# Four gated layers on one core: layer 3's expert rows written plainly to rows of their own and added at the end, and layer 0's router fed from the normalised rows

## What is computed

```
layer 0:  x += tanh(g) * attention(normalised x)                 # 4 sequences of 256
          probs = softmax(norm(x) @ gate_w.T); top 8 of 64 experts, at most 128 tokens each
          x += tanh(g) * sum over the 8 of  prob * expert(norm(x))
layer 3:  mixing with a state space (as in layer 1)
          score = sigmoid(norm(x) @ gate_w.T); top 4 of 32 experts, no limit
          weights = softmax of the 4 logits
          x += tanh(g) * sum over the 4 of  weight * expert(norm(x))
          # expert e: (96 + 128) wide; its second part is shared by two experts
```

## Time and profile before

| | us |
|---|---|
| median of three timed runs (1319.25 to 1321.8) | 1319.86 |
| the profiled execution, device time | 1314.2 |
| its span, first to last instruction | 1312.4 |
| PE busy in the span | 1082.1 (82%) |
| DVE busy | 872.4 (66%) |
| POOL busy | 709.7 (54%) |
| ACT busy | 666.2 (51%) |
| POOL's gathers of layer 3 (L2385, x63) | 61.8 |
| POOL's scatters of layer 3 (L2376, x63) | 100.0 |

### The profile page before, as it was taken

How to read it: one execution, slowest core, us unless ns; L and a number is a source line. 1 busy time by engine, 2 the same in 40 slices (tenths; PEclk the granted TensorE clock), 3 DMA queues, 4 the chain that set the end, 5 groups by cost and what they waited for, 6 DMA issues and landing times.

```text
span 1312.4 us, 18185 instructions
## 1 busy us (share of the span) xinstructions
PE 1082.1 (82%) x5380; PEld 841.4 (64%) x5381; DVE 872.4 (66%) x1543; ACT 666.2 (51%) x1702; POOL 709.7 (54%) x480
## 2 busy tenths in 40 slices
PE   6646668887765988999999999799999737999992
PEld 3525656766623655888888888665555536888781
DVE  4645989898869895566566665859997782332221
ACT  4275245454464214787777777467662125333330
POOL 1002878888733223444554445429996105888873
PEclk9768789999977998999999999979999757999996
DMA  6391789988550003111011110305443992555556
GB/s 184 95 212 59 180 217 322 269 248 217 102 146 1 0 1 95 56 50 53 22 49 55 51 51 1 101 1 150 148 137 75 282 220 65 82 83 83 82 78 130
DMA packets 141109, 146.06 MB, mean 111 GB/s; under 512 B 34180, under 2 KB 127356, under 8 KB 141028
## 3 DMA queue, kind: packets, MB, share of 16 engines
q1 hardware_dynamic: 115556, 110.71, 29.2%
q0 software_dynamic: 24384, 33.31, 15.2%
q10 hardware_dynamic: 1088, 1.05, 0.2%
HBM read 119.04 MB, written 25.99 MB: 111 GB/s over the span
## 4 chain that ended last, share of the span: by engine, by line
PE 45%; POOL 15%; DVE 15%; issue 12%; ACT 6%; DMA 6%; SPq 0%; ACTq 0%; POOLq 0%; DVEq 0%
PE bank L1608 4%; PE bank L1671 4%; PE bank L1704 4%; PE bank L1693 4%; PE bank L2472 4%; POOL f_sums L1039 3%; POOL arena L1025 2%; PE bank L1597 2%; PE bank L2138 2%; PE bank L1626 2%; PE bank L1682 2%; POOL y L2385 2%; POOL arena L585 2%; DMA f_sums<-arena,put 2%; DMA e_sums<-ctxT,put 2%
## 5 line engine op out<-in xcount | busy, mean ns | idle before, releaser
L565 DVE TENSOR_TENSOR_SCAN arena<-arena 128x1024 f32<-128x1024 f32 x64 | 155.3, 2426 | 8.3 <-DVE arena L554 3.9
L1039 POOL DMA_INDIRECT f_sums<-arena,put x64 | 126.7, 1980 | 23.6 <-issue 17.7
L585 POOL TENSOR_TENSOR arena<-arena 128x1024 f32<-128x1024 f32 x32 | 82.4, 2575 | 89.7 <-DVE arena L565 89.7
L1025 POOL DMA_INDIRECT arena<-y_rows,slots x64 | 79.6, 1244 | 81.6 <-DVEq L1232 60.7
L2376 POOL DMA_INDIRECT e_sums<-ctxT,put x63 | 100.0, 1587 | 24.0 <-issue 15.5
L2472 PE MATMUL bank<-arena,ssm_y 128*128 x504 | 109.7, 362 | 2.2 <-issue 1.3
L543 ACT ACTIVATE arena<-arena,ssm_A 128x255 f32<-128x255 f32 x256 | 107.9, 498 | 1.7 <-DVE arena L487 1.5
L2138 PE MATMUL bank<-yT,arena 128*128 128x512 f32 (+1 forms) x224 | 105.8, 618 | 2.2 <-ACT arena L2069 2.2
L595 PE MATMUL bank<-arena,ident 128*128 128x256 f32 x256 | 69.3, 418 | 40.7 <-DVE arena L585 37.2
L554 DVE TENSOR_TENSOR arena<-arena 128x1024 f32<-128x1024 f32 x64 | 94.4, 1475 | 0.0
L2385 POOL DMA_INDIRECT y<-y_rows,slots x63 | 61.8, 982 | 59.6 <-DVEq L2656 40.7
(11 more groups left out here) (342 smaller groups left out, 2792.2 us busy)
## 6 DMA issues: line engine op xcount, KB each, us to landing
arena<-bc_rows SPq DMA_DIRECT2D x64, 512.0 KB, 5.4
arena<-in_L_ffn_w_gate_dram SPq DMA_DIRECT2D x16, 256.0 KB, 3.7
arena<-in_L_ffn_w_up_dram SPq DMA_DIRECT2D x16, 256.0 KB, 4.5
arena<-in_L_ffn_w_down_dram SPq DMA_DIRECT2D x16, 256.0 KB, 5.5
x<-in_L_ffn_w_gate_dram SPq DMA_DIRECT2D x16, 256.0 KB, 3.8
y<-in_L_ffn_w_up_dram SPq DMA_DIRECT2D x16, 256.0 KB, 4.4
yT<-in_L_ffn_w_down_dram SPq DMA_DIRECT2D x16, 256.0 KB, 6.1
arena<-in_L_ffn_Wd_dram SPq DMA_DIRECT2D x1, 3072.0 KB, 18.1
```

The lines of the kernel that those rows point to most:

```text
L565: nc.vector.tensor_tensor_scan(ssm_h[:, j % 2, :], ssm_decay[:, j % 2, :], ssm_in, 0.0, ALU.mult, ALU.add).then_inc(s_ssm_h, 1)
L585: ops.tensor_tensor(ssm_hC_buf[:, j % 2, :], ssm_h[:, j % 2, :], ssm_C[:, g % 2, :], ALU.mult).then_inc(s_ssm_hC, 1)
L1025: nc.gpsimd.indirect_dma_start(out=f0_xg[:, n % RING, e, :], out_offset=None, in_=y_rows, in_offset=bass.IndirectOffsetOnAxis(ap=slots[:, ...
L1039: nc.gpsimd.indirect_dma_start(out=f0_sums[m % SUMS], out_offset=bass.IndirectOffsetOnAxis(ap=put[:, m:m + 1], axis=0), in_=f0_ye[:, n % R ...
```

## The change

Two things are changed.

**Layer 3's sums.** e_sums is replaced by one DRAM tensor e_rows of 4 x 1024 + 64 x 128 rows. The table that PE makes holds 4 x token + k + 1 in place of the token's number; the product with the one-hot factor moves from ACT to DVE, since it differs over k. DVE first writes put and shifts it right by two for slots. Unused slots go to the rows behind the 4096. The scatter is a plain indirect DMA, and waits neither for the scatter of t - 2 nor for a first copy of x. The two clearing transfers for e_sums[1], the last rows of both, and the copy of x are gone. At the end SP reads 8 parts of 512 KB (4 neighbouring rows, 4 KB, for each partition), DVE makes three additions for each token tile (128x512, 128x256, 128x256), and SP stores 8 parts.

**Layer 0's router.** rows_turn and its logits leave the attention loop. The logits come from y after the normalisation, by norm_pe (four transposes, a copy by ACT and the products, for each pair of tiles, on banks 0 and 1) at the head of f0_pe; the scale rstd goes. The attention loop on DVE now runs two taps per sequence, behind the division instead of before it, and so all eight taps of both halves. ACT runs ssm_u_act and ssm_A_act straight behind the attention, ahead of the copies and the exponentials of the router.

```diff
@@ l0x_pe @@
             for b in range(B):
                 if b >= 2:
                     l0x_pe_energy(pe, b)
                 if b >= 1:
                     l0x_pe_out(pe, b - 1)
-                if b >= 2:
-                    rows_turn(b - 2)
             l0x_pe_out(pe, B - 1)
-            rows_turn(B - 2)
-            for b in range(B - 1):
-                rows_logits(b)
-            rows_turn(B - 1)
-            rows_logits(B - 1)
-            logits.last.then_inc(s_f0_logit, 1)
@@ l0x_act @@
-                if b >= 2:
-                    rows_turn_act(act, b - 2, 1, (6, 7))
             l0x_act_turn(act, B - 1)
-            for b in range(B - 2, B):
-                rows_turn_act(act, b, 1, (6, 7))
+            ssm_u_act(act, 0)
+            ssm_A_act(act)
@@ l0x_dve @@
-                ssm_conv_dve(dve, 0, 0, (b,))
                 dve.wait_ge(s_l0_exp, TPB * (b + 1))
...
                 last.then_inc(s_l0_att, 1)
+
+                ssm_conv_dve(dve, 0, b // 2, range(2 * (b % 2), 2 * (b % 2) + 2))
                 if b >= 1:
                     l0x_dve_add(dve, b - 1)
@@ f0_sp @@
-            for rows in f0_sums[1:] + e_sums[1:]:
+            for rows in f0_sums[1:]:
...
-            for rows in f0_sums + e_sums:
+            for rows in f0_sums:
@@ f0_pe @@
+            logits = pair_logits(bank[2], E0, gwT)
+            norm_pe(pe, 1, 1, logits)
+            logits.last.then_inc(s_f0_logit, 1)
             ssm_dt_pe(pe, 0)
@@ f0_act_eng @@
+            norm_act(act, 1)
             act.wait_ge(s_f0_top, 1)
...
-                                            bias=f0_top[:, i:i + 1], scale=rstd[:, i:i + 1], accum_out=f0_sum[:, i:i + 1])
+                                            bias=f0_top[:, i:i + 1], accum_out=f0_sum[:, i:i + 1])
             last.then_inc(s_f0_exp, 1)
-            ssm_A_act(act)
-            ssm_u_act(act, 0)
             ssm_dbl_act(act, 0)
@@ f0_dve @@
             norm_dve(dve, 1)
-            ssm_conv_dve(dve, 0, 1, range(DC))
@@ e_sp @@
-            sp.wait_ge(s_z_x, 2 * B)
-            sp.dma_start(e_sums[0][0:T, :].rearrange("(i p) d -> p i d", p=P), x[:, :, :]).then_inc(s_e_init[0], 16)
...
-            for b in range(B):
-                tiles = slice(TPB * b, TPB * (b + 1))
-                for dst, rows in ((x, e_sums[0]), (e_more, e_sums[1])):
-                    sp.dma_start(dst[:, tiles, :], rows[0:T, :].rearrange("(i p) d -> p i d", p=P)[:, tiles, :]
-                                 ).then_inc(s_e_more[b][0], 16)
+            for i in range(NT):
+                sp.dma_start(e_more[:, i, :, :], e_rows[i * P * K3:(i + 1) * P * K3, :].rearrange("(p k) d -> p k d", k=K3)
+                             ).then_inc(s_e_back[i][0], 16)
@@ e_pool, scatter(t) @@
                 wait(pool, s_e_ye, t + 1)
-                if t >= 2:
-                    wait(pool, s_e_st[(t - 2) % 4], 16 * ((t - 2) // 4 + 1))
-                if t == 0:
-                    wait(pool, s_e_init, 16)
                 nc.gpsimd.indirect_dma_start(
-                    out=e_sums[t % 2], out_offset=bass.IndirectOffsetOnAxis(ap=put[:, t:t + 1], axis=0),
-                    in_=e_ye[:, t % 4, :], in_offset=None, oob_is_err=True, compute_op=ALU.add).then_inc(s_e_st[t % 4][0], 16)
+                    out=e_rows, out_offset=bass.IndirectOffsetOnAxis(ap=put[:, t:t + 1], axis=0),
+                    in_=e_ye[:, t % 4, :], in_offset=None, oob_is_err=True).then_inc(s_e_st[t % 4][0], 16)
@@ e_act @@
-                nc.scalar.activation(e_rhs[:, i % 2, :, 0:TILES], e_ot[:, i % 2, :, :], ACT.Copy, scale=token_1[:, i:i + 1])
@@ e_dve @@
+                wait(dve, s_e_ot, i + 1)
+                V.tensor_tensor(e_rhs[:, i % 2, :, 0:TILES], e_ot[:, i % 2, :, :],
+                                e_tok[:, i, :].unsqueeze(2).to_broadcast([P, K3, TILES]), ALU.mult)
...
-            dve_link(V.tensor_scalar(slots[:, :], bank[5][:, 0:TILES], 1.0, 0.0, ALU.subtract, ALU.max))
+            dve_link(V.tensor_scalar(put[:, :], bank[5][:, 0:TILES], 1.0, 0.0, ALU.subtract, ALU.max))
+            dve_link(V.tensor_scalar(slots[:, :], put[:, :], K3.bit_length() - 1, None, ALU.logical_shift_right))
...
+            for i in range(NT):
+                wait(dve, s_e_back[i], 16)
+                four = e_more[:, i, :, :]
+                dve_link(V.tensor_tensor(four[:, 0:2, :], four[:, 0:2, :], four[:, 2:4, :], ALU.add))
+                dve_link(V.tensor_tensor(four[:, 0, :], four[:, 0, :], four[:, 1, :], ALU.add))
+                V.tensor_tensor(x[:, i, :], x[:, i, :], four[:, 0, :], ALU.add).then_inc(s_e_x[0], 1)
```

More of the change, by code:

```diff
@@ L710, in l0x_pe @@
             pe.wait_ge(s_sp_pad, 4)
-            logits = pair_logits(bank[2], E0, gwT)
-            def rows_turn(b):
-                pe.wait_ge(s_l0_x, b + 1)
-                rows_turn_pe(pe, b, 1, (6, 7))
-            def rows_logits(b):
-                pe.wait_ge(s_yT, NT // 2 + b + 1)
-                logits(b)
             for b in range(B):
@@ L843, in flamingo_kernel @@
         f0_sums = [nc.dram_tensor(f"f0_sums{e}", [T + CAP, D], F32, kind="Internal").ap() for e in range(SUMS)]
-        e_sums = [nc.dram_tensor(f"e_sums{e}", [T + CAP, D], F32, kind="Internal").ap() for e in range(2)]
+        e_rows = nc.dram_tensor("e_rows", [4 * T + E0 * CAP, D], F32, kind="Internal").ap()
         at = 0
@@ L919, in flamingo_kernel @@
         s_f0_clear = sem("s_f0_clear")
-        CLEARS = 8
+        CLEARS = 5
         s_f0_more = [sem(f"s_f0_more{b}") for b in range(B)]
@@ L944, in f0_const_pool @@
             nc.gpsimd.iota(iota_c[:, :], [[1, CAP]], base=0, channel_multiplier=0, allow_small_or_imprecise_dtypes=True)
+            nc.gpsimd.iota(e_tok[:, :, :], [[P * K3, NT], [1, K3]], base=1, channel_multiplier=K3,
+                           allow_small_or_imprecise_dtypes=True)
+            nc.gpsimd.iota(e_none[:, :], [[P, TILES]], base=K3 * T + 1, channel_multiplier=1, allow_small_or_imprecise_dtypes=True)
             nc.gpsimd.iota(token_1[:, :], [[P, NT]], base=1, channel_multiplier=1,
@@ L1187, in f0_dve @@
             norm_dve(dve, 1)
-            ssm_conv_dve(dve, 0, 1, range(DC))
             dve.wait_ge(s_f0_logit, 1)
-            dve_link(nc.vector.tensor_reduce(f0_top[:, :], bank[2][:, :].rearrange("p (i e) -> p i e", i=NT), AX_X, ALU.max,
-                                             negate=True))
-            nc.vector.tensor_tensor(f0_top[:, :], f0_top[:, :], rstd[:, :], ALU.mult).then_inc(s_f0_top, 1)
+            nc.vector.tensor_reduce(f0_top[:, :], bank[2][:, :].rearrange("p (i e) -> p i e", i=NT), AX_X, ALU.max,
+                                    negate=True).then_inc(s_f0_top, 1)
             dve.wait_ge(s_f0_exp, 1)
@@ L2277, in flamingo_kernel @@
         assert at <= ARENA
-        e_more = area(0, NT, D)
+        e_more = area(0, NT, K3, D)
         XR = 8
@@ L2328, in flamingo_kernel @@
         s_e_ld = (s_x_w[0], 16 * H // 2)
-        s_e_more = [(s, 16 * SUMS) for s in s_f0_more]
+        s_e_back = [(s, 16 * SUMS) for s in s_f0_more] + [(s, 16 * B * GB) for s in s_ssm_B + s_ssm_C]
         s_e_x = (s_f0_x, B)
+        e_tok = sb("e_tok", [P, NT, K3])
+        e_none = sb("e_none", [P, TILES])
         EL = 14
@@ L2654, in e_dve @@
             wait(dve, s_e_place, NT)
-            dve_link(V.tensor_scalar(slots[:, :], bank[5][:, 0:TILES], 1.0, 0.0, ALU.subtract, ALU.max))
+            dve_link(V.tensor_scalar(put[:, :], bank[5][:, 0:TILES], 1.0, 0.0, ALU.subtract, ALU.max))
+            dve_link(V.tensor_scalar(slots[:, :], put[:, :], K3.bit_length() - 1, None, ALU.logical_shift_right))
             dve.sem_inc(s_e_slots[0], 1)
-            dve_link(V.tensor_scalar(slot_none[:, :], bank[5][:, 0:TILES], 0.0, none_row[:, 0:1], ALU.is_equal, ALU.mult))
+            dve_link(V.scalar_tensor_tensor(out=slot_none[:, :], in0=bank[5][:, 0:TILES], scalar=0.0, in1=e_none[:, :],
+                                            op0=ALU.is_equal, op1=ALU.mult))
             V.scalar_tensor_tensor(out=put[:, :], in0=bank[5][:, 0:TILES], scalar=-1.0, in1=slot_none[:, :],
@@ L2681, in e_dve @@
             e_steps(dve, step)
-            for b in range(B):
-                wait(dve, s_e_more[b], 32)
-                rows = x[:, TPB * b:TPB * (b + 1), :].rearrange("p a n -> p (a n)")
-                more = e_more[:, TPB * b:TPB * (b + 1), :].rearrange("p a n -> p (a n)")
-                V.tensor_tensor(rows, rows, more, ALU.add).then_inc(s_e_x[0], 1)
+            for i in range(NT):
[4 more added lines that the diff above has]
+                V.tensor_tensor(x[:, i, :], x[:, i, :], four[:, 0, :], ALU.add).then_inc(s_e_x[0], 1)
         s_out = sem("s_out")
@@ L2693, in store_sp @@
             rows = out.rearrange("b (h p) d -> p (b h) d", p=P)
-            for b in range(B):
-                wait(sp, s_e_x, b + 1)
-                sp.dma_start(rows[:, TPB * b:TPB * (b + 1), :], x[:, TPB * b:TPB * (b + 1), :]).then_inc(s_out, 16)
-            sp.wait_ge(s_out, 16 * B)
```

(4 more changed lines are left out.)

1 line of the change is left out of this document (removed).

## The result

Timed beside each other nine times, the kernel after takes 1327.29 us in the median (1323.8 to 1329.12) and the kernel before 1320.34 (1318.62 to 1323.25): a ratio of 1.0045, with a 95% interval of 1.0033 to 1.0057. The forecast was 1305.6. On one of theirs, called E, the same two programs came to 1292.79 (two runs) and 1315.27 us, 0.9821 (0.976 to 0.9881).

A forecast was written before the change was run, and what follows sets the result against it. No engine is busy throughout; the chain of waits counts, in layer 3's experts on PE until 1189, then POOL. The terms -15.7 + 6.5 + 0.9 - 6.0 = -14.3 us take the median from 1319.9 to 1305.6, range 1299 to 1317.

The forecast's parts named there:

- Part 1: Layer 3's experts: a plain scatter costs POOL 0.99 us, not 1.59, and the last landing comes 15.7 us earlier.
- PE then keeps its pace.: Layer 3's experts: with POOL at 2.58 us a tile, PE holds 2.82, its last product ending at 1279.0.
- the gathers and the 32 pairs follow as before: Layer 0's experts: after the earlier routing this stage runs unchanged, so the -6.0 us is passed on.
- Part 2: The end of the kernel: reading back 4.2 MB for 2.1 MB adds 6.5 us after the last landing.
- late as feared: Reading back: last part in at +16.0 us, DVE about as late; loads alone at 244 GB/s would make it +9.5.
- Part 3: Layer 3's routing: DVE gains 0.42 us a tile, ACT loses 0.51; +0.9 us in all, bounds 0 and +2.
- Part 4: Layer 0's router: later logits but earlier Silu and state-space products, -6.0 us, bounds -4.6 and -9.3.
- a time before 83: Layer 0's routing: ACT's first tile, forecast at 85.3, coming this early would say PE had its full clock.
- A: Layer 3's experts: the plain scatter keeps its 1.59 us; total -2.6 us, 1317.3, chance 15%.
- C: Layer 3's experts: the plain write costs POOL more than the accumulating one; at 1.98 us, 1341.5; chance 4%.
- B: Layer 0 gives nothing, as something unseen holds the start of the pairs; total -8.3 us, 1311.6, chance 6%.
- D: Layer 3's experts: POOL is freed, but the four e_ye buffers still hold PE; no chance of its own.

The follow-up runs named there:

- e14: The kernel before, unchanged, run on chip E for its profile: 1316.46 us, 1.0007 of before.
- e17: The kernel after, unchanged, on chip E: 1292.79 us from two runs, 0.9821 of before.
- e12: The kernel before with compute_op=ALU.add left out of layer 3's scatter, so rows overwrite each other, on chip D: 1328.2 us, 1.0047 of before.
- e2: The kernel before with the product with the token's number (L2528) moved from ACT to DVE, on chip A: 1315.34 us, 1.0004 of before.
- e3: The kernel before with layer 0's part of the change alone, on chip A: 1309.56 us, 0.9962 of before.
- e16: The kernel before with layer 0's part of the change alone, on chip E: 1307.55 us, 0.996 of before.
- e4: The kernel before with layer 3's part of the change alone, on chip A: 1303.44 us, 0.9911 of before.
- e1: The kernel after with 8 more instructions (16 waits long reached) on ACT ahead of layer 3's first turned copy, on chip A: 1298.68 us, 0.9865 of before.
- e8: The kernel after with every scatter of layer 3 issued one gather later on POOL, on chip C: 1319.91 us, 0.9997 of before.

## Why the prediction was wrong, point by point

**Part 1, the step that failed: "PE then keeps its pace."** On the chip of the result PE's signals came up to 3.6 us late, PE then idled and ran on at a granted clock of 0.50, and a tile took 3.29 us in place of 2.82. The price of the plain scatter was right (0.988 for 0.99), and so was what the transfers said of it: in the stretch above q0 has 5574 packets for 117 gathers and plain scatters of after, 48 each, where an accumulating one made 144. Why an accumulating one keeps POOL itself 0.6 us longer no run shows. Right as well was what it does where PE's signals come on time. On chip E, with before beside it, it is 189.3 us from the first gather of layer 3 to the last landing, against 206.4 (1093.51 to 1299.95 in e14): -17.2 for the -15.7 forecast; 1.1 of the difference is the landing, 2.41 us and not 3.5. The marks of e14, then of e17 (POOL's first gather and the last scatter's way to its landing):

```profile
1093.51 1.07 POOL L2385 DMA_INDIRECT y<-y_rows,slots  x1 [41.05 <-DVEq L2656]
...
1296.20 3.75 DMA e_sums<-ctxT,put
```

```profile
1084.92 1.07 POOL L2362 DMA_INDIRECT y<-y_rows,slots  x1 [41.82 <-DVEq L2636]
...
1271.77 2.41 DMA e_rows<-ctxT,put
```

On the chip of the result, turns 2 and 62 of after (against the earlier trace rows) lie 197.4 us apart, 3.29 a tile:

```profile
1098.51 0.53 PE L2426 MATMUL bank<-ident,y 128*128 128x128 f32 x2
...
1295.86 0.38 PE L2426 MATMUL bank<-ident,y 128*128 128x128 f32 x2
```

The forecast took 2.82 from a profile in which PE was not disturbed once, and asked only what POOL and the four buffers might do to it. On this chip part 1 came out at +11.3 for -15.7: 27.0 of the 27.4 us between the forecast's -14.3 and the +13.1 of the two profiles. The profile of before is itself of the other kind of chip, and so the forecast missed the measured difference of the medians, +7.0, by 21.3.

The forecast did note that the profiled execution lay 5.7 us under the median, and added them back as a constant. It was the one sign that the profile and the times were of different conditions: 1314.2 lies outside the 1319.25 to 1321.8 of the three timings.

Whether before has late signals in layer 3 too on such a chip, and POOL's slower pace hides them, or has none there, stays open: no profile of it fell on one. In layer 0 it has them, by e12, and up to the sixth scatter they cost some 4.4 us there. Before takes 4 to 7 us longer on chips B, C and D than on A and E, so if the 4.4 last to the end, little is left that its layer 3 could lose. The forecast's "the gathers and the 32 pairs follow as before" doesn't hold on such a chip either: from the first gather to the last scatter of layer 0 it is 253.3 us in after and 249.0 in the profile of before. That fits the 3.0 us that are left at layer 3's first gather of the 8.7 by which after was ahead at layer 0's, though the profiles on chips A and E alone spread from 243.3 to 252.7 there.

**Part 2, the reading back.** The mechanism was right, the size (+6.5) a little high: from the last landing to the end 18.3 us in after and 18.1 in e17, against 13.5 and 12.7 in before, so +4.8 and +5.5 for +6.5. The loads were not late as feared. DVE's three additions follow each other without a wait from 1311.13, 1.52 a tile for the 1.63 taken.

**Part 3, layer 3's routing.** The last products of the logits, in before and in after:

```profile
1051.26 3.46 PE L258 MATMUL bank<-e_gwT,yT 128*128 128x32 f32 x16
```

```profile
1047.11 3.46 PE L258 MATMUL bank<-e_gwT,yT 128*128 128x32 f32 x16
```

From their end to the first gather it is 37.2 us in before (1054.72 to 1091.94), 38.3 in after (1050.57 to 1088.91), +1.1 for +0.9. e2 shows that the moved product is not to be seen in the time.

**Part 4, layer 0's router.** PE did not have its full clock: after 2.77 us of idle time it was granted 1.00 from 56 to 57 and 0.50 from 58 to 67, and from the first turn (55.80) to the end of the last 16 products of the logits (61.70 and 3.52) it took 9.4 us for the 9.3 forecast. At 0.50 these 16 took 0.22 each; before's 24 in 2.79 us, at 1.00, took 0.12. What came sooner was the end of the attention loop: its last addition starts at 53.07, in before at 54.59, -1.5 for the +0.4 forecast. So L430 started at 65.14, not 66.9, and took 5.01 us, not 5.50. ACT's first routing tile came at 82.95, not 85.3; the forecast had named a time before 83 as the sign of a full clock, and here it was none. One execution doesn't measure the rest: the first gather of layer 0 lies between 105.7 and 115.3 in the 13 profiles with this part, 111.6 in the mean, and between 116.2 and 118.8, mean 117.1, in the 7 without: -5.5. All of these moments lie ahead of the first late signal. The time agrees, -5.0 (e3) and -5.3 (e16) by the ratios, for the -6.0 forecast. So the -8.7 of the first two profiles (118.36 to 109.65) was partly spread, and on chips A and E nothing of it had to be given back later.

**The rivals.** None was it. A and C priced the scatter too high. B fell with e3 and e16. D looked at what could hold PE and found only the buffers. The missing rival was: PE loses its pace once it, and not POOL, sets it. The forecast's sum was right in sign for chips A and E (-14.3 forecast; -11.8 for e4, which lacks layer 0's part, -16.6 for e1, -22.5 for e17), wrong for the first chip, B and D; on C only shifted copies ran. The parts as measured on E add up to -17.2 + 5.5 + 1.1 - 5.3 = -15.9, just inside e17's interval of two runs (-15.7 to -31.6); the 6.6 us more of its median are not explained.

## What to carry to other kernels

A slower engine at the bound may hide what the next engine does badly; whether POOL did so in before is open. Before counting on the next one's pace, look at whether it was ever alone at the bound in the conditions of the timed runs, not only of the profiled one; if the profiled time lies outside the timed ones, the profile may be of something else. And when an edit that can't matter (e1's eight waits) seems to cure a loss, run the uncured kernel again beside it: here it was the chip or its state, and the group on chip A without e2 and e4 would have seemed to prove a wrong theory. A choice between versions that rests on one chip can have the wrong sign on the next: after and its copy e1 are the fastest kernels on chips A and E, and after is slower than before on the first chip, B and D, as three of its four copies are on C (e8, with another order on POOL, is even with before).

## What the runs showed of the hardware

The same program takes 1292.79 us on one chip and 1325.96 to 1330.02 on others, and no execution of it lies more than 4.6 us from the median of its chip. The difference in layer 3's experts is that the signals of PE's finished work reach ACT, DVE and POOL up to 4.1 us late, 22 to 39 times on ACT alone in 62 tiles, often just behind the end of PE's next product (0.67 us at tile 15, 0.25 at tile 23, where the product ends at 1176.44 and the Silu starts at 1176.69), while PE's records run on evenly. It was seen in all ten profiles with plain scatters on the first chip, B, C and D and in none of the four on chips A and E. In layer 0's experts, with accumulating scatters, the same ten have late signals and the nine on A and E have none.

That PE works on and only its signals are held can be seen, although the ends of matmuls are modelled. The trace holds the moments at which PE's semaphores were raised. In e17 they lie 0.01 to 0.02 us behind the modelled ends. In after, around tile 15, PE's five pieces of work end at 1144.93 (products), 1145.14 (turn of h), 1146.01 (down), 1146.23 (next turn) and 1147.75 (next products), and their signals come at 1148.39, 1148.44, 1148.50, 1148.54 and 1148.63: nothing for 3.4 us, then all five within 0.24 us. Eight products take 1.68 us at a granted clock of 1.00 (the eight at 1146.07), so the second eight can't have been done in these 0.24. Behind every one of the six large late Silus of after the next Silu comes 0.80 to 1.23 us later, and not 2.82.

Fetching of instructions doesn't show in it: the queue q8 has 40 packets in the whole run on either chip, and in the stretch above both have 4, and q14 3 (here after, e17 has the same packets and bytes):

```profile
q8 instruction: 4, 0.07, 0.1%
q14 instruction: 3, 0.02, 0.0%
```

What holds the signals is open. Shifts of 1, 2 and 8 instructions, another order on POOL and a PE program without its reads don't remove it. Nor is it shown that the chip is what decides: only E was used in two groups, a few minutes apart, and so a lasting state of the chip or a property of it can't be told apart. On the chips with late signals some records of PE's semaphore updates are missing (in after 55, 60 and 57 are left of those of 63 turns, gate and up products and down products, in e17 all); whether the recording plays a part was not tried.
